# GpSimd in place of VectorE for the two 16-bit parts of the softmax shift in a fused SSM, FFN and attention kernel, with fillers in five waits of TensorE

## The chip, the cores and the metric

The kernel runs on one core of a Trainium2 chip. A core has five engines with queues of their own, each of which works through its instructions in order: TensorE (PE; its weight loads are shown as PEld), VectorE (DVE), ScalarE (ACT), GpSimd (POOL) and SyncE (SP), which here starts the DMA transfers. Engines wait for one another by semaphores. The metric is the device time of one execution in microseconds (us); lower is better.

## What is computed

The input `x` has 4096 tokens of 256 channels in float32. Four layers follow one another, each with a layer norm ahead of it and the residual added behind it: a gated recurrent block, a feed-forward block with token shift, causal attention, and the same feed-forward block again.

```python
x = x + s4_block(layernorm(x))      # gates i, f, o = sigmoid(x W + b), s = tanh(x W + b), h = f * h + i * s, y = o * h
x = x + ffn(layernorm(x))           # sigmoid(xr W_r) * (relu(xk W_k)^2 W_v), xr and xk mix a token with the one before
x = x + attention(layernorm(x))     # 16 heads of 16 channels, causal, over all 4096 tokens
x = x + ffn(layernorm(x))

# attention, for each block of queries:
scores = einsum('bhqd,bhkd->bhqk', qc, k) * scale
scores = where(causal_mask, -inf, scores)
p = softmax(scores - max(scores))
oc = einsum('bhqk,bhkd->bhqd', p, v)
```

## The kernel before

Tokens go through the feed-forward and recurrent layers in 16 units of 256. Attention is cut into 32 **steps**: `STEPS` pairs each of the 8 chunks of 512 queries with each of the 4 groups of 4 heads. Step 0 is chunk 0 with group 0, step 10 chunk 2 with group 2. Within a step, the keys are walked over in tiles of 128.

The softmax needs the largest score of a query ahead of the exponentials, and it gets it by computing the scores twice. First TensorE makes score blocks with the queries on the partitions (`max`, L1746, with the mask added by L1753 on the diagonal), and VectorE reduces each 128x512 block to one column of `span_max` (`reduce`, L1537). At the end of a step VectorE does three small things: `neg` (L1543) reduces `span_max` to `neg_max`, the negative maximum of 128 queries x 16 (four query tiles and four heads); `part0` (L1550) writes its scaled value in float16, the first part of the shift; `part1` (L1555) writes what float16 lost, the second part. `shift` on TensorE (L1761, four matmuls with an identity) turns both parts into rows, ScalarE copies them out (`shift.copy`, L1272), and four DMAs (`place`) put them below the queries in `q_stack`. The second computation of the scores (`scores`, L1778, keys on the partitions) so comes out already shifted, ScalarE exponentiates it (`exp`, L1281 and L1292), GpSimd masks the tiles on the diagonal (`mask`, L1147), and `pv` (L1799) multiplies by the values, summing in a PSUM bank of its own. `out` (L1808) and two VectorE instructions (L1561 and L1569) normalize the result.

Everything else runs between these: the projections (L1595 and L1603), transposes (L1588, L1642, L1808), tanh and copies on ScalarE (L1186 to L1265), and on GpSimd the layer norms of the middle units (L978 to L985, for the recurrent block L1037 and L1039 on top), affine steps, additions and masks.

**What sets the order.** `schedule()` is a planner that runs when the kernel is built. It plays all work through with costs (`COST`) and weights (`WORTH`), and gives out one list, `ORDER`. Each engine's program walks over that list and emits the entries that are its own, so the order on each engine is fixed. `followed()` says what an entry must come behind. `part0` and `part1` are entries of VectorE in the planner, at 180 ns each. A matmul bank in PSUM (seven of them) is claimed by TensorE when its last reader is done (`claim`). `shift` waits for `shift_ready`, and everything behind it on TensorE waits with it. `settle` on GpSimd makes an instruction wait for the end of the one before. `warm` entries put transposes of an identity (L1620, **fillers**) into long planned waits of TensorE before the first and behind the last attention work; nobody reads their result.

## Time and profile before

| | us |
|---|---|
| median of 3 runs | 1751.62 |
| lowest, highest | 1751.35, 1752.64 |
| profiled execution | 1752.51 |
| its span, first to last instruction | 1750.8 |

| engine | busy us | share of the span |
|---|---|---|
| TensorE | 1711.9 | 98% |
| VectorE | 1507.0 | 86% |
| ScalarE | 1343.5 | 77% |
| GpSimd | 687.9 | 39% |

Busy time is the union of an engine's instructions. For TensorE their ends are modelled and matmuls overlap, so a busy share near 100% does not mean that it runs at its peak. The chain is the work that ended last, followed back from the last instruction, at each step to what released it or to the instruction before it on its engine.

### The profile page before, as it was taken

Reading aid. Unit: us, or ns where it says so; the run is one execution under the profiler, and the core shown is the slowest. Engines: PE = TensorE matmul, PEld = TensorE weight load, DVE = VectorE, ACT = ScalarE, POOL = GpSimd, SP = SyncE. Lnnn points to the kernel's source line nnn. Section 1 sums busy time; section 2 is a strip of 40 time slices with the busy share of each in tenths; the row PEclk is TensorE's granted clock in tenths of the full one; section 3 lists DMA queues with packets and bytes.
Section 4 is the critical chain, followed back from the end, with each engine's and each line's share of the span. In section 5 each row is a group of like instructions: output and inputs, shape, how many; then the busy total and the mean of one; then the engine's idle time right before and its main releaser. Section 6 shows DMA issues by size and latency. Waiting matters only on the chain.

```text
span 1750.8 us, 45629 instructions
## 1 busy us (share of the span) xinstructions
PE 1711.9 (98%) x18228; PEld 641.7 (37%) x18228; DVE 1507.0 (86%) x2975; ACT 1343.5 (77%) x2796; POOL 687.9 (39%) x994
## 2 busy tenths in 40 slices
PE   8999999999999999999999999999999999999997
PEld 6654444334433333334333333333333322323224
DVE  6778978986899999998999999999999999999702
ACT  3336577767677878876888688898888899998994
POOL 3348766578572453428332625211322120102221
PEclk9999999999999999999999999999999999999999
DMA  4133121003102010020000020000002000000000
GB/s 113 53 71 60 30 43 34 19 19 61 30 18 48 13 30 13 8 48 25 6 24 2 24 32 6 18 18 2 1 19 35 18 2 6 14 1 2 14 7 13
DMA packets 57000, 43.71 MB, mean 25 GB/s; under 512 B 8788, under 2 KB 56788, under 8 KB 56788
## 3 DMA queue, kind: packets, MB, share of 16 engines
q1 hardware_dynamic: 54548, 39.75, 9.5%
q8 instruction: 144, 2.36, 0.6%
q10 hardware_dynamic: 2240, 1.05, 0.4%
q14 instruction: 68, 0.56, 0.1%
HBM read 24.00 MB, written 16.25 MB: 23 GB/s over the span
## 4 chain that ended last, share of the span: by engine, by line
PE 72%; DVE 15%; ACT 4%; POOL 3%; issue 2%; DMA 0%; ACTq 0%; POOLq 0%; DVEq 0%
PE psum L1799 22%; PE psum L1746 14%; PE psum L1778 13%; DVE span_max L1537 12%; PE psum L1595 10%; PE psum L1603 9%; ACT probs L1281 2%; PE psum L1588 2%; ACT probs L1292 1%; PE psum L1753 1%; PE psum L1808 1%; DVE rows L1476 1%; DVE small L1386 0%; POOL small L979 0%; POOL rows L985 0%
## 5 line engine op out<-in xcount | busy, mean ns | idle before, releaser
L1537 DVE TENSOR_REDUCE span_max<-psum 128x1 f32<-128x512 f32 (+3 forms) x2304 | 1313.9, 635 | 100.0 <-PE psum L1746 71.8
L1281 ACT ACTIVATE probs<-psum 128x512 f32<-128x512 f32 (+2 forms) x2178 | 1054.1, 571 | 165.9 <-PE psum L1778 162.4
L1799 PE MATMUL psum<-probs,v_aug 128*17 128x512 f32 (+3 forms) x4608 | 564.5, 562 | 1.7 <-ACT oT L1301 1.3
L1746 PE MATMUL psum<-k_stack,q_stack 48*128 48x512 f16 (+3 forms) x2304 | 528.8, 364 | 4.4 <-DVE span_max L1537 3.3
L1778 PE MATMUL psum<-q_stack,k_stack 50*128 50x512 f16 (+3 forms) x2304 | 508.3, 364 | 4.4 <-ACT probs L1292 1.2
L1778 PEld LDWEIGHTS psum<-q_stack,k_stack 50*128 50x128 f16 x2304 | 147.7, 93 | 378.6 <-ACT probs L1281 272.8
L1746 PEld LDWEIGHTS psum<-k_stack,q_stack 48*128 48x128 f16 x2304 | 154.9, 93 | 298.8 <-DVE span_max L1537 223.4
L1147 POOL TENSOR_SCALAR_AFFINE_SELECT probs<-probs 128x512 f32<-128x512 f32 x128 | 81.2, 637 | 319.0 <-ACT probs L1281 288.9
L1799 PEld LDWEIGHTS psum<-probs,v_aug 128*17 128x17 f32 x4608 | 78.2, 95 | 134.9 <-issue 114.1
L1186 ACT ACTIVATE rows<-psum,cols 128x256 f32<-128x256 f32 x128 | 53.8, 479 | 56.8 <-PE psum L1595 53.2
L1753 PE MATMUL psum<-mask_keys,mask_rows 64*128 64x64 bf16 x1024 | 93.8, 189 | 0.0
L1753 PEld LDWEIGHTS psum<-mask_keys,mask_rows 64*128 64x128 bf16 x1024 | 76.6, 95 | 28.8 <-issue 0.2
L1140 POOL TENSOR_TENSOR rows<-rows 128x512 f32<-128x512 f32 x26 | 33.1, 1273 | 108.6 <-ACT rows L1223 108.6
L1386 DVE BATCH_NORM_STATS2 small<-rows 128x6 f32<-128x256 f32 x160 | 59.3, 412 | 15.5 <-POOL rows L1124 8.3
L1595 PE MATMUL psum<-rows,w_k 128*32 128x256 f32 x1024 | 68.7, 386 | 3.3 <-DVE rows L1503 2.3
L985 POOL TENSOR_SCALAR rows<-rows,small 128x256 f32<-128x256 f32 x124 | 67.8, 554 | 6.8
L1088 POOL TENSOR_TENSOR rows<-rows 128x512 f32<-128x512 f32 x26 | 27.0, 1040 | 106.2 <-ACT rows L1200 106.2
L1603 PE MATMUL psum<-w_r,rows 128*32 128x256 f32 x1024 | 67.9, 383 | 0.7 <-POOL rows L1101 0.2
L1603 PE MATMUL psum<-w_v,rows 128*32 128x256 f32 x1024 | 67.7, 383 | 0.7 <-DVE span_max L1537 0.4
L1135 POOL TENSOR_SCALAR rows<-rows 128x512 f32<-128x512 f32 x26 | 16.4, 630 | 130.4 <-ACT rows L1207 130.3
L1561 DVE RECIPROCAL inv_sum<-psum 128x16 f32<-128x16 f32 x32 | 8.0, 250 | 67.6 <-PE psum L1808 67.2
L979 POOL TENSOR_TENSOR small<-small 128x2 f32<-128x2 f32 x80 | 57.9, 723 | 6.7
(139 smaller groups left out, 1543.7 us busy)
## 6 DMA issues: line engine op xcount, KB each, us to landing
q_stack<-q_parts SPq DMA_DIRECT2D x192, 32.0 KB, 1.9
k_stack<-k_parts SPq DMA_DIRECT2D x42, 128.0 KB, 4.8
rows<-in_x SPq DMA_DIRECT2D x16, 256.0 KB, 2.8
q_parts<-rows SPq DMA_DIRECT2D x32, 128.0 KB, 2.0
k_parts<-rows SPq DMA_DIRECT2D x32, 128.0 KB, 2.3
out<-rows SPq DMA_DIRECT2D x16, 256.0 KB, 2.2
x_rows<-rows SPq DMA_DIRECT2D x14, 256.0 KB, 2.1
rows<-x_rows SPq DMA_DIRECT2D x14, 256.0 KB, 2.7
```

Source lines behind the costliest of these rows:

```text
L979: return nc.gpsimd.tensor_tensor(rstd[:, ln], var_eps[:, ln], minus_half, ALU.pow)
L985: ins = nc.gpsimd.tensor_scalar(dst[:, j], src[:, j], neg_mean[:, ln, j:j + 1], rstd[:, ln, j:j + 1], ALU.add, ALU.mult)
L1147: nc.gpsimd.affine_select(out=tri, in_=tri, compare_op=ALU.is_ge, fill=0.0, base=0, pattern=[[0, HG], [1, P]], channel_multiplier=-1).then ...
L1281: act.activation(probs[:, tile % PROBS, i, q0:], bank(b)[:, q0:], ACT.Exp, scale=SCALE / QK_SCALE).then_inc(exp_done, 1)
L1386: ins = nc.vector.bn_stats(stats[:, ln, j], src[:, j])
L1537: nc.vector.tensor_reduce(span_max[:, s % SPAN_RING, row:row + 1, k0 // SPAN:k0 // SPAN + 1], bank(b)[:, 0:k1 - k0], AX.X, ALU.max).then_i ...
L1595: ins = nc.tensor.matmul(bank_chan(b)[c:c + COLUMNS, e], w[:, k, e * P + c:e * P + c + COLUMNS], src[:, k], start=(k == 0), stop=(k == CT ...
L1603: ins = nc.tensor.matmul(bank_tok(b)[c:c + COLUMNS, j], src[:, k, j * P + c:j * P + c + COLUMNS], w[:, k], start=(k == 0), stop=(k == CT - 1))
L1746: ins = nc.tensor.matmul(bank(b)[:, 0:k1 - k0], q_stack[row:row + SCORE_ROWS, s % Q_RING, u, qt * P:(qt + 1) * P], k_stack[row:row + SCORE ...
L1753: ins = nc.tensor.matmul(bank(b)[:, k:k + HALF], mask_rows[row:row + HALF, n], mask_keys[row:row + HALF], start=False, stop=(n == 1))
L1778: nc.tensor.matmul(bank(b)[:, q0:], k_stack[row:row + STACK, g * PAIRS + u, j * P:(j + 1) * P], q_stack[row:row + STACK, s % Q_RING, u, q0 ...
L1799: ins = nc.tensor.matmul(pv_bank[32 * h:32 * h + VW, q0:], v_aug[:, j, g * HG + h, :], probs[:, tile % PROBS, h, q0:], start=(j == 0), sto ...
```

## The change

The two parts of the shift are written by GpSimd. VectorE still computes `neg`. At the place of `part1` in the order GpSimd waits for `neg`, scales `neg_max` in place, copies it to float16 as the first part, and subtracts that from the scaled value for the second, each of the three waiting for the end of the one before. `neg` now also waits for the parts of the step before, as GpSimd reads and writes `neg_max`. The planner is not told: in it `part0` and `part1` are still two entries of VectorE, so all other work stands in the same order.

The planner also gets a second rule for fillers: a planned wait of TensorE over 300 ns, after the first `max` and before the first `pv`, gets one filler for every 110 ns beyond 190.

```diff
@@ schedule(), the planner
         if e == "PE" and gap > 1000 and (not summed or summed == len(TILES)):
             order.append(("warm", int(WARM_SHARE * (gap - 400) / (WARM if free["PE"] else WARM_COLD))))
+        elif e == "PE" and gap > 2 * SWITCH + WARM and maxed and not summed:
+            order.append(("warm", int((gap - 2 * SWITCH) / WARM)))
@@ semaphores
-        neg_ready, part_ready, shift_ready, shift_copied = (sem(n) for n in ("neg_ready", "part_ready", "shift_ready",
-                                                                              "shift_copied"))
+        neg_ready, shift_ready, shift_copied = (sem(n) for n in ("neg_ready", "shift_ready", "shift_copied"))
@@ GpSimd
+                elif op[0] == "part1":
+                    s = op[1]
+                    pool.wait_ge(neg_ready, s + 1)
+                    if s >= 2:
+                        pool.wait_ge(full["shift"], s - 1)
+                    settle(nc.gpsimd.tensor_scalar(neg_max[:], neg_max[:], 1.0 / ROW_UNIT, None, ALU.mult))
+                    settle(nc.gpsimd.tensor_copy(shift_parts[:, s % 2, :, 0], neg_max[:]))
+                    nc.gpsimd.tensor_tensor(shift_parts[:, s % 2, :, 1], neg_max[:], shift_parts[:, s % 2, :, 0],
+                                            ALU.subtract).then_inc(shift_ready, 1)
@@ VectorE
                     dve.wait_ge(span_reduced, 2 * MAXIMA_UPTO[s])
+                    if s:
+                        dve.wait_ge(shift_ready, s)
                     spans = ((STEPS[s][1] + 1) * CHUNK + SPAN - 1) // SPAN
                     nc.vector.tensor_reduce(neg_max[:], span_max[:, s % SPAN_RING, :, 0:spans], AX.X, ALU.max,
                                             negate=True).then_inc(neg_ready, 1)
-                elif op[0] == "part0":
-                    s = op[1]
-                    dve.wait_ge(neg_ready, s + 1)
-                    if s >= 2:
-                        dve.wait_ge(full["shift"], s - 1)
-                    nc.vector.tensor_scalar(shift_parts[:, s % 2, :, 0], neg_max[:], 1.0 / ROW_UNIT, None,
-                                            ALU.mult).then_inc(part_ready, 1)
-                elif op[0] == "part1":
-                    s = op[1]
-                    dve.wait_ge(part_ready, s + 1)
-                    nc.vector.scalar_tensor_tensor(out=shift_parts[:, s % 2, :, 1], in0=neg_max[:],
-                                                   scalar=1.0 / ROW_UNIT, in1=shift_parts[:, s % 2, :, 0],
-                                                   op0=ALU.mult, op1=ALU.subtract).then_inc(shift_ready, 1)
@@ TensorE, op "warm"
-                    if scores:
+                    if scores == HG * len(TILES):
                         pe.wait_ge(o_copied, len(STEPS))
                     else:
                         pe.wait_ge(pv_cleared, 1)
```

On GpSimd, in step 10 (chunk 2, third group of heads), before the change. L982 to L985 normalize a unit, L1037 and L1039 finish the recurrent block's norm, L1079 copies a column, and the next normalization follows:

```order
L982 TENSOR_SCALAR small<-small 128x2
L978 TENSOR_SCALAR small<-small 128x2
L979 TENSOR_TENSOR small<-small 128x2
L985 TENSOR_SCALAR rows<-rows,small 128x256 x2
L1037 TENSOR_TENSOR rows<-rows,gamma_b 128x512
L1039 TENSOR_TENSOR rows<-rows 128x512
L1079 COPY rows<-small 128x2
L982 TENSOR_SCALAR small<-small 128x2
```

The same place after the change (line numbers of the changed kernel, two higher):

```order
L984 TENSOR_SCALAR small<-small 128x2
L980 TENSOR_SCALAR small<-small 128x2
L981 TENSOR_TENSOR small<-small 128x2
L987 TENSOR_SCALAR rows<-rows,small 128x256 x2
L1039 TENSOR_TENSOR rows<-rows,gamma_b 128x512
L1041 TENSOR_TENSOR rows<-rows 128x512
L1127 TENSOR_SCALAR neg_max<-neg_max 128x16
L1128 CAST shift_parts<-neg_max 128x16
L1129 TENSOR_TENSOR shift_parts<-neg_max,shift_parts 128x16
L1081 COPY rows<-small 128x2
L984 TENSOR_SCALAR small<-small 128x2
```

Three instructions have come in behind the last addition of the norm and ahead of the copy; nothing else has moved.

On TensorE, between the maxima of step 0, with the difference of before and after. L1588 transposes a unit's rows, L1746 and L1753 are a `max` block and its mask, L1620 are the fillers:

```order
+L1620 MATMUL psum<-ident 128x128 x5
+L1746 MATMUL psum<-k_stack,q_stack 128x256
+L1753 MATMUL psum<-mask_keys,mask_rows 128x64 x2
+L1746 MATMUL psum<-k_stack,q_stack 128x256
+L1753 MATMUL psum<-mask_keys,mask_rows 128x64 x2
+L1588 MATMUL psum<-ident,rows 128x128 x4
+L1746 MATMUL psum<-k_stack,q_stack 128x384
+L1753 MATMUL psum<-mask_keys,mask_rows 128x64 x2
+L1746 MATMUL psum<-k_stack,q_stack 128x384
+L1753 MATMUL psum<-mask_keys,mask_rows 128x64 x2
+L1620 MATMUL psum<-ident 128x128 x3
```

The rows between the fillers also stand in the kernel before, in the same order. In all five places there are 2, 5, 3, 2 and 2 fillers, 14 together.

## Rows read from the trace of the kernel before

**Rows 1.** The page: busy time by engine; the last chain by engine.

```profile
PE 1711.9 (98%) x18228; PEld 641.7 (37%) x18228; DVE 1507.0 (86%) x2975; ACT 1343.5 (77%) x2796; POOL 687.9 (39%) x994
...
PE 72%; DVE 15%; ACT 4%; POOL 3%; issue 2%; DMA 0%; ACTq 0%; POOLq 0%; DVEq 0%
```

**Rows 2.** VectorE's groups by shape: busy us, mean ns, idle before.

```profile
L1550 DVE TENSOR_SCALAR shift_parts<-neg_max 128x16 f16<-128x16 f32 x32 | 12.3, 383 | 0.3
...
L1555 DVE SCALAR_TENSOR_TENSOR shift_parts<-neg_max,shift_parts 128x16 f16<-128x16 f32 x32 | 8.3, 259 | 0.4
```

**Rows 3.** The chain, steps 4, 5, 10 and 27: start us, us, what.

```profile
188.50 0.61 DVE shift_parts L1550
...
210.52 0.39 DVE shift_parts L1550
...
364.84 0.20 PE psum L1761 x4
...
1338.23 0.68 DVE shift_parts L1550
```

**Rows 4.** Timeline of step 13: start us, us, instruction, [idle before <-releaser].

```profile
499.29 0.22 POOL L978 TENSOR_SCALAR small<-small 128x2 f32<-128x2 f32 x1
...
499.59 0.71 POOL L979 TENSOR_TENSOR small<-small 128x2 f32<-128x2 f32 x1
...
502.94 1.26 POOL L1039 TENSOR_TENSOR rows<-rows 128x512 f32<-128x512 f32 x1
503.15 1.10 DVE L1555 SCALAR_TENSOR_TENSOR shift_parts<-neg_max,shift_parts 128x16 f16<-128x16 f32 x1
...
504.39 0.38 PE L1761 MATMUL psum<-ident_h,shift_parts 128*8 128x128 f16 x4 [1.41 <-DVE shift_parts L1555]
```

**Rows 5.** GpSimd's groups by shape.

```profile
L1101 POOL TENSOR_TENSOR rows<-rows 128x512 f32<-128x512 f32 x52 | 56.9, 1094 | 4.3
...
L982 POOL TENSOR_SCALAR small<-small 128x2 f32<-128x2 f32 x62 | 15.2, 246 | 33.3 <-DVE small L1401 19.8 <-DVE rows L1462 5.4 <-POOL rows L1110 2.9
...
L1079 POOL COPY rows<-small 128x2 f32<-128x2 f32 x32 | 6.4, 199 | 0.0
```

**Rows 6.** Timelines of TensorE and GpSimd, step 10.

```profile
364.66 0.39 PE L1761 MATMUL psum<-ident_h,shift_parts 128*8 128x128 f16 x4
...
365.87 1.09 POOL L1039 TENSOR_TENSOR rows<-rows 128x512 f32<-128x512 f32 x1
```

**Rows 7.** The same, steps 6 and 27.

```profile
234.60 1.10 POOL L985 TENSOR_SCALAR rows<-rows,small 128x256 f32<-128x256 f32 x2
...
234.91 0.39 PE L1761 MATMUL psum<-ident_h,shift_parts 128*8 128x128 f16 x4
...
1340.15 1.09 POOL L1101 TENSOR_TENSOR rows<-rows 128x512 f32<-128x512 f32 x1
...
1340.74 0.39 PE L1761 MATMUL psum<-ident_h,shift_parts 128*8 128x128 f16 x4
```

**Rows 8.** The same, step 11.

```profile
395.06 1.16 POOL L1130 TENSOR_TENSOR rows<-rows 128x512 f16<-128x512 f32 x1
...
395.39 0.39 PE L1761 MATMUL psum<-ident_h,shift_parts 128*8 128x128 f16 x4
...
397.79 1.16 POOL L1130 TENSOR_TENSOR rows<-rows 128x512 f16<-128x512 f32 x1 [1.44 <-ACT rows L1245]
```

**Rows 9.** TensorE's timeline, 88 to 113 us; a window's busy times and clock; the chain.

```profile
90.87 1.20 PE L1620 MATMUL psum<-ident 128*128 128x128 f32 x9
...
111.04 0.28 PE L1746 MATMUL psum<-k_stack,q_stack 48*128 48x256 f16 x1 [0.66 <-DVE span_max L1537]
...
core 0: us, PE busy (x) PEld busy (x) DVE busy (x) ACT busy (x) POOL busy (x), PEclk, DMA share, GB/s
...
112.30:119.10 6.80, 6.37 (x60) 3.27 (x60) 6.80 (x18) 1.09 (x2) 1.27 (x1) 0.50 0.01 2
...
114.65 4.97 PE psum L1595 x48
...
120.30 2.73 PE psum L1595 x48
```

## The prediction

> **What bounds the kernel now.** I first read the page's busy shares [rows 1]: TensorE 98%, VectorE 86%, ScalarE 77%, GpSimd 39%. A busy TensorE is not one at its peak, so I next read the chain that ended last, by engine: 72% TensorE, 15% VectorE, 3% GpSimd [rows 1]. TensorE's fixed order carries the end, with detours over VectorE where a bank waits for a maximum. A chain piece that starts when its releaser ends has no slack: delay it and the rest of the chain moves by as much. Shorten it, and only as much is won as the next-longest path allows. So each of the 32 steps is read at one place, `neg`, the two parts, and the `shift` matmuls on TensorE, and I ask whether that place is on the chain.
>
> **What VectorE gives up.** Two instructions a step go: L1550, 32 at a mean of 383 ns, 12.3 us, and L1555, 32 at 259 ns, 8.3 us; 20.6 us together [rows 2]. Off the chain this is worth nothing. Following the chain piece by piece I find 18 pieces of these two lines, the first and the last in [rows 3], about 10.5 us in sum. Their means are well over their usual length because some wait for GpSimd: in step 13 L1555 starts at 503.15 and lasts 1.10, to 504.25, while GpSimd's L1039 runs from 502.94 for 1.26, to 504.20 [rows 4]; L1550 before it took 1.15 beside L1037 in the same way. By the Trainium skill, SBUF — State Buffer, section "SBUF: two separate sides", VectorE and GpSimd share one pair of ports, which one instruction holds to its end while the other blocks. The trace agrees: the long part ends 0.05 us behind GpSimd's instruction. That rule alone would speak for the move, as it makes both parts cost nothing on VectorE.
>
> Of the ten or so steps in which the chain runs through these pieces, most need the parts for their own shift, so the path only moves over to GpSimd. In four it goes on into reductions: step 5 (0.39 for L1550 [rows 3], and 0.97 for the L1555 behind it), and steps 14, 15 and 16, read in the same way (0.64, 0.54 and 0.78). At most 1.36 + 1.96 = 3.3 us. I take 1.0 and 1.4, that is about seven tenths, because TensorE follows closely behind. **Gain 2.4 us (0 to 3.3).**
>
> **What GpSimd takes on.** Three instructions a step, with a wait between each: a tensor_scalar, a cast, a subtraction, all 128x16. The trace has none of these on GpSimd. The nearest rows are 246 ns for a 128x2 tensor_scalar, 199 ns for a 128x2 copy, 1094 ns for a 128x512 tensor_tensor [rows 5]. 128x16 lies next to the small ends: 0.26 + 0.21 + 0.28 = 0.75. The hand-over from L978 to L979 costs 499.59 - 499.29 - 0.22 = 0.08 [rows 4], twice 0.16. From the last part to TensorE it was 504.39 - 503.15 - 1.10 = 0.14 [rows 4]. So about 1.03 us pass from when GpSimd is free to when `shift` starts (0.8 at the copy's price for all three, 1.3 with one at a third of the big subtraction). Added up that is some 29 us on an engine 39% busy; mostly it hides in GpSimd's waits.
>
> What does not hide is the queue. GpSimd runs its list in order, and the parts stand where `part1` stood, behind work that in this trace is later than the plan. So `shift` starts at the end of GpSimd's preceding instruction plus 1.03, if that is later than before:
> Step 10: L1039 ends 365.87 + 1.09 = 366.96, shift 367.99 instead of 364.66: +3.3 [rows 6]. `neg` had ended 5 us before; all that time GpSimd is in two normalizations.
> Step 6: L985 ends 235.70, shift 236.73 instead of 234.91: +1.8 [rows 7].
> Step 27: L1101 ends 1341.24, shift 1342.27 instead of 1340.74: +1.5 [rows 7]. Step 21, read alike: +1.3.
> Step 13: L1039 ends 504.20, 505.23 instead of 504.39: +0.85 [rows 4].
> Step 11: L1130 ends 396.22, 397.25 instead of 395.39: +1.9. Here the chain is on GpSimd, but its next L1130 at 397.79 waits for ScalarE's L1245, which stands behind the shift's copy L1272: the delay comes through whole [rows 8].
> Five more steps, read alike: 2 (0.3), 3 (0.95, the three instructions stand directly in a chain of GpSimd's instructions), 4 (0.3), 7 (0.6), 22 (0.55).
> In the other 21 steps GpSimd is done in time, or the shift had been waiting behind other matmuls. In all 3.3 + 1.8 + 1.3 + 1.5 + 0.85 + 1.9 + 2.7 = **13.3 us lost**. `shift` is on the chain, or a bank wait from it, in each of these (step 10's piece at 364.84 is in [rows 3]), so I count them whole. Behind the waiting `shift` on TensorE stand score, maximum and value matmuls, and VectorE and ScalarE live on those. With 0.8 or 1.3 for the three instructions the sum is 10.8 or 16.3. GpSimd's masks behind the parts come up to 1.03 us later in a few steps; the value matmuls that need them come after the equally late `shift`: 0 to 1, taken as 0. The new wait of `neg` on the parts of the step before, with reductions queued behind it on VectorE, costs nothing: the parts are done in the few us named here, and two `neg` lie many reductions apart.
>
> **The fillers.** Five places get 14 transposes between them; nine in a row take 1.20 us [rows 9], so 2, 5, 3, 2 and 2 of them take 0.27, 0.67, 0.40, 0.27 and 0.27. TensorE's idle time there is 0.66 where five go [rows 9] and 0.41, 0.29, 0.26 and 0.28 in the others, counted from a matmul's modelled end, which lies 0.1 and more behind its last column, so they fit within about 0.05. So they cost nothing. What they can bring: the granted clock is 0.50, TensorE's lower level of 1.2 GHz, from 112.3 to 119.1, right behind those idle times. 48 matmuls of L1595 take 4.97 us there against 2.73 just after [rows 9]: 2.2 us, with the four transposes ahead of them 2.8 at most. But VectorE is busy for 6.80 of these 6.80 us [rows 9] and would take over as the bound: I take half, 1.4 us (0 to 2.8). By the Trainium skill, TensorE: Matmul & The Clock Gate, section "HAM oscillation — how this bites in real kernels", short idle pieces between groups of matmuls can lower the clock again, so filling them should hold it; the row of 0.50 behind the waits agrees, but no run here shows yet that these few fillers are enough.
>
> **Sum.** 1750.8 + 13.3 - 2.4 - 1.4 = 1760.3 for the span. The profiled execution took 1752.51 with a span of 1750.8, so 1.7 lies around it: 1762.0. The median of the three runs is 0.9 below that execution: **1761.0 us**, 0.54% slower.
>
> **Rivals.**
> 1. GpSimd is on time, VectorE's relief stays. The late GpSimd is that of one execution; once work starts earlier, if GpSimd's backlog at steps 6, 10, 11, 21 and 27 moves ahead of `neg`, the stalls fall and the gains stand: 1751.6 - 3.3 - 2.8 = 1745.5. For it: GpSimd is idle 61% of the span. Against it: in step 10 GpSimd has no gap worth the name in the 6 us before, and what feeds it (VectorE's statistics) does not come sooner. It decides where less than 1 us of the stalls is left. 0.10.
> 2. A draw. Only the two largest stalls, steps 10 and 11 (5.2 us), are smaller, because they hang on a backlog of one stretch, and gains are at their upper ends: 1751.6 + 8.1 - 6.1 = 1753.6. 0.18.
> 3. The clock falls in the new stall. In step 10 TensorE would stand idle for about 3 us; the 1.41 ahead of step 13's shift [rows 4] kept the clock, but at 112.3 it fell behind waits of 0.66 and less [rows 9]. A stretch like that of [rows 9] costs another 2.2 to 3.4: 1764. 0.16.
> 4. The 128x16 instructions cost 1.3 us or more: 1764 to 1766. 0.08.
> The forecast has 0.48. The range of 1753 to 1768 takes in the forecast's own ends (10.8 to 16.3 lost, 0 to 6.1 gained), rivals 3 and 4 and most of the draw. A measurement of this kernel can tell about 0.2%, 3.5 us, from no change. Faster by more than that is rival 1, 0.10; within it lies most of rival 2 and the low edge of the forecast, 0.18; slower 0.72.
>
> **What the changed profile would show.** Right: `shift` waits for GpSimd's subtraction, in steps 10, 6, 11, 13, 21 and 27 above all, for some 12 us; GpSimd's three instructions at about 0.26, 0.21 and 0.28 us; VectorE's busy time down by about 20 us with more idle time in its place; the granted clock 1.00 from 112 to 119. Wrong: small waits of `shift` for GpSimd, which would be rival 1 or 2; a second stretch of half clock behind 365 us, rival 3; or GpSimd instructions of 0.4 us and more, rival 4.

## The result and the profile after

| | before | after |
|---|---|---|
| median | 1752.13 us (4 runs) | 1771.76 us (4 runs) |
| lowest, highest | 1751.35, 1752.76 | 1770.12, 1773.39 |
| profiled execution's span | 1750.8 | 1769.3 |

The ratio is 1.0113, with a 95% interval of 1.0101 to 1.0125. The change costs 19.6 us. The forecast was a loss of 9.4 us and a range that ended at 1768: the sign was right, the size half of what came, and the time lies outside the range.

The first view is the page of the kernel after, busy time by engine; it answers to [rows 1].

```profile
PE 1716.5 (97%) x18242; PEld 642.0 (36%) x18242; DVE 1492.8 (84%) x2911; ACT 1345.0 (76%) x2796; POOL 708.5 (40%) x1090
```

VectorE lost 14.2 us of work, GpSimd gained 20.6, and TensorE has 4.6 us more on its hands although it does only 14 short transposes more. That last number is the first hint of a slower clock: the same matmuls took longer. VectorE's two instructions a step were 20.6 us; its other instructions took some 6 us longer in sum, 4.6 of them in the 128x512 reductions of `span_max` (1305.2 us before, 1309.9 after), and no run here tells why.

GpSimd's groups by shape (busy us, mean ns | idle before) show the three new instructions, which answer to [rows 5]:

```profile
L1127 POOL TENSOR_SCALAR neg_max<-neg_max 128x16 f32<-128x16 f32 x32 | 8.7, 273 | 120.8 <-DVE neg_max L1556 120.8
...
L1129 POOL TENSOR_TENSOR shift_parts<-neg_max,shift_parts 128x16 f16<-128x16 f32 x32 | 7.5, 236 | 2.7
L1128 POOL CAST shift_parts<-neg_max 128x16 f16<-128x16 f32 x32 | 6.5, 203 | 2.2
```

273, 203 and 236 ns stand where I had put 260, 210 and 280. The 120.8 us ahead of L1127 are time in which GpSimd waits for `neg`: in most steps it really is early. Who waits for the last of the three (idle us of the waiting engine, times), from the view of that one line:

```profile
L1129 POOL TENSOR_TENSOR shift_parts<-neg_max,shift_parts x32: 220/226/562, 123.9 to 1672.4; 128x16 f16<-128x16 f32 x32
...
who waited for it (us, times):
  PE psum L1761: 18.4, 13
```

So in 13 of 32 steps `shift` found GpSimd late, for 18.4 us in all. Of these 1.6 us were there before as waits for VectorE, 1.41 in step 13 [rows 4] and 0.15 in step 7; **16.8 us are new**. (A third wait of before, 0.42 us in step 4, is gone.) Nobody but `shift` waited, so the new wait of `neg` for the parts cost nothing, as forecast. The largest new one is in step 10. The timeline of that place (start us, us, instruction, [idle before <-releaser]) answers to [rows 6]:

```profile
371.02 1.26 POOL L1039 TENSOR_TENSOR rows<-rows,gamma_b 128x512 f32<-128x512 f32 x1
372.37 1.09 POOL L1041 TENSOR_TENSOR rows<-rows 128x512 f32<-128x512 f32 x1
373.43 0.28 POOL L1127 TENSOR_SCALAR neg_max<-neg_max 128x16 f32<-128x16 f32 x1
373.77 0.20 POOL L1128 CAST shift_parts<-neg_max 128x16 f16<-128x16 f32 x1
374.06 0.22 POOL L1129 TENSOR_TENSOR shift_parts<-neg_max,shift_parts 128x16 f16<-128x16 f32 x1
374.43 0.38 PE L1761 MATMUL psum<-ident_h,shift_parts 128*8 128x128 f16 x4 [3.05 <-POOL shift_parts L1129]
```

This is the forecast's picture: the two big norm instructions end at 373.46, and 0.97 us later `shift` starts, where I had said 1.03 and a loss of 3.3.

**Where the loss comes in.** Both traces have all matmuls in the same order (fillers aside), so each matmul can be set against its own twin. The table gives, for `shift`, the start after less the start before, in us:

| step | 0 | 2 | 3 | 4 | 5 | 6 | 7 | 9 | 10 | 11 | 13 | 14 | 20 | 21 | 27 | 31 |
|---|---|---|---|---|---|---|---|---|---|---|---|---|---|---|---|---|
| later by | -2.0 | -0.9 | +0.4 | +1.8 | +1.1 | +2.8 | +4.6 | +6.5 | +9.8 | +13.1 | +13.7 | +16.8 | +16.1 | +17.4 | +18.5 | +18.5 |

It is a staircase that climbs, with small steps down (0.7 us at step 5, 0.7 between steps 14 and 20). Nothing large is given back, and it ends at the 18.5 us by which the span is longer. Two kinds of step make it: the waits of `shift`, and stretches in which TensorE runs on its lower clock. The windows (us; busy us and count of each engine; granted clock; DMA share; GB/s) answer to [rows 9]:

```profile
core 0: us, PE busy (x) PEld busy (x) DVE busy (x) ACT busy (x) POOL busy (x), PEclk, DMA share, GB/s
...
112.30:119.10 6.80, 6.54 (x106) 3.54 (x107) 6.80 (x19) 1.33 (x3) 2.23 (x4) 1.00 0.01 2
188.00:191.40 3.40, 3.37 (x31) 1.63 (x28) 1.55 (x5) 1.43 (x3) 2.54 (x6) 0.50 0.29 80
239.20:242.60 3.40, 3.40 (x36) 1.35 (x32) 3.04 (x8) 2.44 (x6) 3.23 (x4) 0.50 0.01 2
375.70:379.10 3.40, 3.40 (x19) 0.58 (x15) 2.19 (x6) 2.17 (x6) 2.85 (x7) 0.50 0.06 7
519.10:522.50 3.40, 3.40 (x25) 0.86 (x21) 3.04 (x6) 3.22 (x8) 3.21 (x6) 0.50 0.01 2
```

The half clock at 112 is gone, as the fillers were meant to bring about, and four new stretches stand elsewhere. Three of them begin 1 to 2 us behind a long wait of `shift`: steps 6 (wait 1.56, shift at 237.66), 10 (3.05, at 374.43) and 13 (2.21, at 518.05). From twin to twin, TensorE falls back by 1.2, 1.3, 1.6 and 1.6 us across the four, 5.7 together, 4.5 of it behind the three waits.

The lead of 2.0 us at step 0 is not the fillers' alone. TensorE was 2.75 us early before step 0's wait of 0.67, and 1.0 of that stood at 112 us, ahead of anything that the fillers' clock could win. Most of it arises at 23 us, where the change has done nothing yet. The rows are from before and then from after:

```profile
23.37 1.97 PE L1720 MATMUL psum<-probs 128*128 128x256 f32 x8 [0.80 <-DVE probs L1332]
...
22.66 1.97 PE L1720 MATMUL psum<-probs 128*128 128x256 f32 x8
```

`e4_clock_fill`, which up to there is the same program as the kernel after, waits 1.15 us at this place, so it is scatter between executions. From 112 to 120 us the lead grows from 1.0 to 2.75, and 1.7 us is what the held clock wins. In sum: scatter -1.0, fillers -1.7, waits +16.8, clock +5.7, and -1.3 for VectorE's relief and all that I can't assign make the 18.5.

### The profile page after: what moved, and what is told of

It is laid out like the page before. It is cut to its first block and busy times, and to the rows that moved or that the text cites. A ratio compares the mean times of both kernels' runs of the same rounds, so it can differ in the third digit from the quotient of the medians.

```text
span 1769.3 us, 45720 instructions
## 1 busy us (share of the span) xinstructions
PE 1716.5 (97%) x18242; PEld 642.0 (36%) x18242; DVE 1492.8 (84%) x2911; ACT 1345.0 (76%) x2796; POOL 708.5 (40%) x1090
## 3 DMA queue, kind: packets, MB, share of 16 engines
q10 hardware_dynamic: 2240, 1.05, 0.4%
## 5 line engine op out<-in xcount | busy, mean ns | idle before, releaser
L1746 PE MATMUL psum<-k_stack,q_stack 48*128 48x512 f16 (+3 forms) x2304 | 528.6, 364 | 2.7 <-DVE span_max L1548 1.6
L1746 PEld LDWEIGHTS psum<-k_stack,q_stack 48*128 48x128 f16 x2304 | 154.4, 94 | 296.0 <-DVE span_max L1548 219.3
L1753 PE MATMUL psum<-mask_keys,mask_rows 64*128 64x64 bf16 x1024 | 94.0, 189 | 0.0
L1753 PEld LDWEIGHTS psum<-mask_keys,mask_rows 64*128 64x128 bf16 x1024 | 76.8, 96 | 29.6 <-issue 0.3
L1151 POOL TENSOR_TENSOR rows<-rows 128x512 f32<-128x512 f32 x26 | 33.1, 1274 | 103.3 <-ACT rows L1234 103.3
L1146 POOL TENSOR_SCALAR rows<-rows 128x512 f32<-128x512 f32 x26 | 16.1, 618 | 115.6 <-ACT rows L1218 115.5
L1100 POOL TENSOR_SCALAR rows<-rows,small,cols 128x256 f32<-128x256 f32 x104 | 58.4, 570 | 1.1
```

The source lines that it names most:

```text
L1100: ins = nc.gpsimd.tensor_scalar(dst[:, k], f_xr[:, k], zero, cols[:, COL[om], k:k + 1], ALU.add, ALU.mult)
L1746: ins = nc.tensor.matmul(bank(b)[:, 0:k1 - k0], q_stack[row:row + SCORE_ROWS, s % Q_RING, u, qt * P:(qt + 1) * P], k_stack[row:row + SCORE ...
L1753: ins = nc.tensor.matmul(bank(b)[:, k:k + HALF], mask_rows[row:row + HALF, n], mask_keys[row:row + HALF], start=False, stop=(n == 1))
```

## The experiments

Theory: `shift` stands in TensorE's fixed order behind GpSimd's in-order queue, each wait comes through whole, and the clock that falls behind the longer waits is a second loss of its own. Rivals: the fillers cost rather than help; VectorE's new order is what costs; or the parts are late for GpSimd's price, not for its place in the queue. Times are medians; ratios are against runs of the kernel before on the same chip in the same job. Where a step is given as late or early, that is the difference in the start of its `shift` to the profiled kernel before, as in the table above.

### The two halves of the change apart

`e1_fillers_only` is the kernel before with the new rule for fillers alone:

```diff
+        elif e == "PE" and gap > 2 * SWITCH + WARM and maxed and not summed:
+            order.append(("warm", int((gap - 2 * SWITCH) / WARM)))
...
-                    if scores:
+                    if scores == HG * len(TILES):
```

> The kernel before with the 14 fillers alone; VectorE writes both parts. Theory (four terms: late GpSimd, clock lost behind the stalls, fillers' gain, little relief): the granted clock stays 1.00 from 112 to 119 us, and the kernel comes out about 1.9 us faster than before, 1750.2 us, by the difference of the two traces at step 0's shift (-2.0 us). Rival (the gain at 112 us is given back later, as VectorE or GpSimd bounds the stretch behind it): within 0.5 us of before.

Measured: 1751.44 us (10 runs) against 1752.51 (19 runs), ratio 0.9997 (0.9987 to 1.0007), so nothing that can be measured. Its windows:

```profile
112.30:119.10 6.80, 6.55 (x106) 3.57 (x108) 6.80 (x20) 1.26 (x3) 2.16 (x4) 1.00 0.01 2
...
184.70:188.10 3.40, 3.37 (x25) 1.56 (x26) 2.20 (x6) 1.48 (x4) 2.20 (x3) 0.50 0.38 106
```

The clock holds at 112, and TensorE then is 2.75 us early through steps 0 to 3, 1.0 of it from before the clock's share, as in the kernel after. A half-clock stretch that the kernel before did not have follows at 185, and at step 4 the lead is 1.75, from step 10 on 1.2 to 1.5. The fillers work where they stand; part of what they win is lost again, and the rest is small against how the kernel before scatters by itself (1749.9 to 1753.9 in these 19 runs). By the time the rival was right, though what gave the gain back was the clock and not another engine.

`e2_parts_only` is the kernel after without that rule. 

> The changed kernel without the five groups of fillers; GpSimd writes both parts. Theory: the loss of the changed kernel (+19.6) plus the fillers' gain of 1.9, so about +21.5 against before, 1773.6 us, with a half-clock stretch at about 112 us again. Rival (the fillers only move the phase of the clock, and it is their doing that it falls at 188, 239, 376 and 519 us): those four stretches are gone, and the kernel is about 5 us faster than the changed one, 1766.

Measured: 1770.04 us (4 runs), ratio 1.0104 (1.0088 to 1.0119), within the interval of the full change. Half clock stands at 111.7 to 118.5, as before, and at 190.2, 241.4, 374.5 and 517.9. Both expectations missed: the kernel is neither 2 us slower than the changed one nor 5 faster. The stretches behind steps 6, 10 and 13 belong to the parts on GpSimd, not to the fillers, and the whole loss is the parts'. The waits of 1.31 and 1.16 us in steps 9 and 14 are not there, nor is step 0's; the section on the prediction comes back to them.

### What the parts cost at all

`e5_no_parts` is `e1_fillers_only` in which nobody writes the parts: VectorE fills both once with zeros, and `shift` waits for `neg` alone. It leaves the two part instructions of all 32 steps out, so its scores are not shifted.

```diff
+            nc.vector.memset(shift_parts[:], 0.0).then_inc(filled, 1)
...
-                elif op[0] == "part0":
...
-                elif op[0] == "part1":
...
-                                            negate=True).then_inc(neg_ready, 1)
+                                            negate=True).then_inc(shift_ready, 1)
```

> The kernel of e1 (fillers alone) with both parts left out: nobody writes them, shift reads zeros, and neg alone releases it, so the scores are exponentiated unshifted. VectorE is relieved of the same two instructions a step and GpSimd gets nothing. Theory (the relief is worth little, because TensorE follows closely behind VectorE): 0.5 to 3 us faster than e1, 1748.5 to 1751. Rival (my 10.5 us of chain pieces are worth their length once no queue of GpSimd takes their place): 8 us or more faster, below 1744.

Measured: 1745.52 us (5 runs) against 1751.94 (15), ratio 0.9963 (0.9949 to 0.9977). No half clock anywhere; the last `shift` is 6.96 early. So to write the parts costs some 6 us against `e1_fillers_only`, and in this order no placing of them on another engine should bring more. That lies between what the two sides had expected, and above the 3.3 us that my prediction gave as the upper bound of VectorE's relief. Of the 5.7 us between the two traces, 1.0 is the stretch at 185 of `e1_fillers_only`, which is not there, and 1.4 the wait of step 13, gone with the parts. The bound counted only the steps in which the chain goes on into reductions, but where the chain goes through the parts into `shift`, leaving them out wins as well. That part is not to be had by moving them: GpSimd's three instructions take 1.0 us of their own there.

### Price or place

`e8_one_more` casts twice, which adds 0.28 us (0.20 and a hand-over) to each step on GpSimd and changes no order:

```diff
-                    settle(nc.gpsimd.tensor_copy(shift_parts[:, s % 2, :, 0], neg_max[:]))
+                    for _ in range(2):
+                        settle(nc.gpsimd.tensor_copy(shift_parts[:, s % 2, :, 0], neg_max[:]))
```

> The changed kernel with the cast on GpSimd done twice, so one more instruction of 0.20 us and one more hand-over of 0.09 us in each step. Theory (the queue position decides, the arithmetic only adds its own length in the 13 steps where shift waits): 13 x 0.29 = 3.8 us slower than the changed kernel, 1775.5, give or take a half-clock stretch of 1 to 2 us. Rival (GpSimd's backlog builds up from instruction to instruction, so small work is multiplied): over 8 us slower than the changed kernel.

Measured: 1775.54 us (4 runs), ratio 1.0139 (1.0124 to 1.0154), 3.8 us over the kernel after, as expected. The trace shows that the agreement is in part luck. In ten of the thirteen late steps the wait is 0.25 to 0.28 us longer, so there the price counts in full. In steps 2, 9 and 14 it is shorter (by 0.56, 1.04 and 0.09), and all waits of `shift` for GpSimd together rose by 1.2 us only, to 19.6. The clock's share is another one too: there are five stretches, at 137.2, 239.6, 372.7, 410.3 and 1362.6, the third 6.9 us long, and none behind step 13, where the wait was longer than in the kernel after:

```profile
520.79 0.38 PE L1762 MATMUL psum<-ident_h,shift_parts 128*8 128x128 f16 x4 [2.46 <-POOL shift_parts L1130]
...
519.00:524.00 5.00, 3.21 (x37) 1.19 (x37) 2.25 (x5) 2.76 (x7) 4.35 (x12) 1.00 0.00 1
```

`e3_parts_at_neg` keeps the price and changes the place. GpSimd's three instructions move to where `neg` stands in the common list, some entries earlier:

```diff
-                elif op[0] == "part1":
+                elif op[0] == "neg":
```

> The changed kernel with GpSimd's three instructions moved up in GpSimd's order to the place of neg, ahead of the one or two entries (a mask, a 5 us z.norm in step 10, an addition) that the order has between neg and part1 in 19 of the 32 steps. Theory (the loss is GpSimd's queue, not its arithmetic): the idle time ahead of shift goes in steps 3, 4, 6, 9, 10, 14 and 27 and shrinks in 2, 7, 11 and 22; it stays in 13 and 21, where the z.norm stands ahead of neg. Stalls fall from 17 to about 5 us, the clock falls at most once or twice, and the kernel takes about 1755. Rival (GpSimd now waits for neg with its own late work behind it, and that hurts as much): 1765 or more.

Measured: 1755.79 us (10 runs), ratio 1.0016 (1.0007 to 1.0026). Some 16 of the 19.6 us are back (17 by the ratios), by a change of one word. Step 10 on GpSimd's timeline, ahead of the two norm instructions now and not behind them:

```profile
363.07 0.28 POOL L1127 TENSOR_SCALAR neg_max<-neg_max 128x16 f32<-128x16 f32 x1
...
366.62 1.28 POOL L1039 TENSOR_TENSOR rows<-rows,gamma_b 128x512 f32<-128x512 f32 x1
367.97 1.09 POOL L1041 TENSOR_TENSOR rows<-rows 128x512 f32<-128x512 f32 x1
```

The waits in steps 2, 3, 6, 9, 10, 14, 22 and 27 are gone. Left are 0.68 in step 0, 0.19 in 7, 0.48 in 11, 1.06 in 21 and, the largest, step 13:

```profile
507.47 0.38 PE L1761 MATMUL psum<-ident_h,shift_parts 128*8 128x128 f16 x4 [2.19 <-POOL shift_parts L1129]
```

That one is followed by one of this kernel's two half-clock stretches, at 508.5. The other, from 136.5 to 143.3, begins with an idle time of 1.22 us, which is the rival's effect in one place: GpSimd writes step 1's parts ahead of a mask now, and `pv` waits for the mask.

```profile
137.82 1.91 PE L1799 MATMUL psum<-probs,v_aug 128*17 128x512 f32 x8 [1.22 <-POOL probs L1158]
```

TensorE goes from 1.8 us early at step 0 to 1.4 late at step 1, which is most of what is left of the loss. So the place in the queue makes most of the loss; the price of the three instructions counts where the place makes them late, with the same three instructions standing earlier the kernel is 3.3 us slower than before, not 19.6.

### Does the clock cost by itself

`e7_step10_only` takes `e1_fillers_only` and gives GpSimd the parts of step 10 alone, at `part1`'s place. One stall, and nothing else changed but that `neg` waits for the parts of the step before:

```diff
@@ GpSimd
+                elif op[0] == "part1" and op[1] == 10:
...
@@ VectorE
+                elif op[0] in ("part0", "part1") and op[1] == 10:
+                    pass
```

> The kernel of e1 with GpSimd writing the parts in step 10 alone, behind its z.norm as in the changed kernel; VectorE writes them in the other 31. Theory (a stall on the chain comes through whole, and the clock falls behind it): one idle time of about 3 us ahead of step 10's shift, +3.2 us at that shift and +1.2 for one half-clock stretch at about 370 us, and nothing given back until the end: 4.4 us slower than e1, 1755.8. Rival (VectorE and ScalarE catch up during the stall, and TensorE gets the time back later): under 1.5 us slower than e1.

Measured: 1757.81 us (5 runs), ratio 1.0035 (1.0021 to 1.0048), 6.4 us over `e1_fillers_only`, 2 more than expected. The stall and the window behind it:

```profile
366.47 0.28 POOL L1127 TENSOR_SCALAR neg_max<-neg_max 128x16 f32<-128x16 f32 x1
...
367.48 0.58 PE L1776 MATMUL psum<-ident_h,shift_parts 128*8 128x128 f16 x4 [3.08 <-POOL shift_parts L1129]
...
366.50:373.30 6.80, 5.82 (x32) 1.50 (x36) 2.80 (x7) 3.30 (x7) 5.35 (x15) 0.50 0.14 39
```

The step before, `shift` was 0.44 early; in step 10 it is 2.82 late, in step 11 5.45, and at the last step 5.35. The stall costs 3.3 us, the clock behind it 2.6 more (the clock had fallen at 366.5, still within the stall, and stayed down for 6.8 us), and in the 21 steps that follow nothing of it comes back. Another 0.8 us against `e1_fillers_only` stands already at step 9, ahead of the stall, and is not the parts'. This is the prediction's third rival in a pure form.

`e4_clock_fill` and `e11_clock_fill_all` are the kernel after with transposes that nobody reads in front of the waiting `shift`, so that TensorE works while it waits, in three steps and in eleven (of the thirteen late ones, all but 0 and 14):

```diff
                     claim(b, shift_copied, s + 1)
+                    for n in range({6: 12, 10: 26, 13: 18}.get(s, 0)):
+                        nc.tensor.transpose(bank(b)[:, 0:P], ident[:], ident[:])
```

(In `e11_clock_fill_all` the numbers are 2: 8, 3: 8, 6: 12, 7: 5, 9: 8, 10: 26, 11: 13, 13: 18, 21: 8, 22: 8, 27: 15.) They do nothing for the parts, which `shift` waits for as before.

> The changed kernel with 12, 26 and 18 transposes ahead of TensorE's wait for the parts in steps 6, 10 and 13, written into the bank that shift then overwrites. They fill the stalls and take no work away. Theory (three of the four half-clock stretches are caused by these idle times and cost 1.4, 1.2 and 2.0 us): the clock stays 1.00 at 239, 376 and 519 us and the kernel is about 4.6 us faster than the changed one, 1767.2. Rival (the stalls alone cost the time and the clock costs nothing, since VectorE or ScalarE bound those stretches): 1771.8, unchanged.

Measured: 1765.55 us (4 runs), ratio 1.0074 (1.0059 to 1.0089), 6.2 us better than the kernel after. Its windows over the three places:

```profile
239.00:243.00 4.00, 4.00 (x64) 2.08 (x63) 3.64 (x9) 3.34 (x8) 3.83 (x6) 1.00 0.03 6
371.00:380.00 9.00, 9.00 (x99) 4.40 (x97) 4.21 (x11) 5.53 (x12) 8.05 (x17) 1.00 0.11 31
512.00:520.00 8.00, 8.00 (x88) 4.40 (x83) 3.89 (x9) 4.94 (x11) 7.19 (x17) 1.00 0.13 31
...
1353.90:1357.30 3.40, 3.38 (x30) 1.30 (x34) 1.67 (x4) 1.82 (x4) 0.43 (x1) 0.51 0.03 7
```

Three stretches are gone, one at 190.0 stayed, and one at 1353.9, in step 27, is new. The gain is above the 4.6 us expected for the clock; in this trace step 14's wait of 1.16 us is not there and step 9's is 0.86 instead of 1.31, with nothing filled in either.

> The changed kernel with fillers ahead of TensorE's wait for the parts in all eleven steps with a stall on the chain (2, 3, 6, 7, 9, 10, 11, 13, 21, 22, 27), in place of the three of e4. Theory (with the clock held the loss is the sum of the stalls alone, and e4's two stretches at 190 and 1354 us were stalls not filled): no half-clock stretch behind 150 us apart from perhaps the one at 190, 1.5 to 2.5 us faster than e4, 1.0062 of before. Rival (the fillers themselves delay shift by the last of them in each step): as e4 or slower.

Measured: 1763.72 us (4 runs), ratio 1.0072 (1.0057 to 1.0087), with one stretch of half clock left, at 187.5. Step 10 on TensorE, and the one window that stayed:

```profile
368.96 3.06 PE L1760 MATMUL psum<-ident 128*128 128x128 f32 x26
...
372.03 0.39 PE L1763 MATMUL psum<-ident_h,shift_parts 128*8 128x128 f16 x4
...
187.50:190.90 3.40, 3.31 (x33) 1.39 (x33) 2.31 (x7) 1.71 (x4) 3.25 (x7) 0.50 0.20 57
```

The 129 transposes that nobody needs, 26 of them in step 10, make the kernel faster. Against the kernel after, 0.41% are won, 7.2 us (the two intervals together leave some 3 us to either side); in the traces the span is 7.5 shorter. Not all of that is the clock: from twin to twin 4.6 us lie in the three stretches, 1.2 are the wait of step 14, which is not there in this trace either, and the rest are small waits. By the times it can't be told from `e4_clock_fill`. What is left is the loss of the other stalls: 0.72%, 12.6 us (10.0 to 15.2), or 11.0 at the last `shift` of the trace.

### A version that uses what was learnt

`e6_split_at_neg` has the fillers, GpSimd's parts at `neg`'s place, and VectorE as before in steps 0, 1, 13 and 21, where `e3_parts_at_neg` still waited or GpSimd was behind:

```diff
@@ GpSimd
+                elif op[0] == "neg" and op[1] not in (0, 1, 13, 21):
...
@@ VectorE
+                elif op[0] in ("part0", "part1") and op[1] not in (0, 1, 13, 21):
+                    pass
```

> The kernel of e3 (GpSimd's three instructions at neg's place), but in steps 0, 1, 13 and 21, where e3 still showed TensorE idle ahead of or around shift, VectorE writes the parts as before. Theory (what is left of the loss in e3 are those queues and the clock lost behind them): the +2.9 us of e3 against before go, and the kernel comes to e1 or up to 1.5 us below it, 1750 to 1751.5. Rival (GpSimd's waits for neg cost something spread over all steps): it stays at 1753 or more.

Measured: 1749.52 us (10 runs), ratio 0.9988 (0.9979 to 0.9997), no half clock anywhere. The page, and the one wait for GpSimd that counts, in step 11:

```profile
PE 1710.0 (98%) x18242; PEld 642.1 (37%) x18242; DVE 1496.1 (86%) x2919; ACT 1343.8 (77%) x2796; POOL 706.6 (40%) x1078
...
394.22 0.38 PE L1776 MATMUL psum<-ident_h,shift_parts 128*8 128x128 f16 x4 [0.50 <-POOL shift_parts L1129]
```

It is the fastest of all versions that compute everything, by 2.1 us against the kernel before. That is less than the 3.5 us (0.2%) that I set as the line for "no change", though the interval lies just under 1. It overlaps that of `e1_fillers_only` (0.9987 to 1.0007), so no run shows that the parts on GpSimd win anything over the fillers alone.

`e9_split2` gives VectorE step 11 too:

> The kernel of e6, with VectorE writing the parts in step 11 as well, where e6 still showed 0.50 us of idle TensorE ahead of shift and lost 1.3 us against the step before. Theory (the chain there runs through ScalarE's shift copy, so the loss comes through whole): about 1.0 us faster than e6, 0.998 of before. Rival (something else costs it there): no difference from e6.

Measured: 1749.57 us (10 runs), ratio 0.9988 (0.9978 to 0.9997). From step 10 to 11 it loses 0.66 us instead of 1.3, but a stretch of half clock at 185.8 comes with it, and the time is the same.

`e10_split_no_fillers` is `e6_split_at_neg` without the rule for fillers:

> The kernel of e6 without the five groups of fillers. Theory, after e1 and e2 had shown less than 0.1% for the fillers: they decide where the clock dips, not by how much in sum; within 0.1% of e6. Rival (their gain of 2 us at 112 us is real here, since e6's trace has no half-clock stretch at all): 2 to 3 us slower than e6, and a half-clock stretch at about 112 us.

Measured: 1750.69 us (10 runs), ratio 0.9998 (0.9988 to 1.0007). The half clock of the kernel before is back:

```profile
111.50:118.30 6.80, 6.34 (x60) 3.20 (x60) 6.80 (x18) 1.03 (x2) 1.28 (x1) 0.50 0.01 2
```

The step from `e10_split_no_fillers` to `e6_split_at_neg` is 1.2 us, about the 1.4 that my prediction gave to the fillers, but the two intervals overlap, so it is an indication and no more. In the traces TensorE wins 2.2 us up to step 0 by the fillers' clock, after 1.0 us of scatter at 23.7 us the other way.

## Why the prediction was half right

The forecast's terms beside what the traces show, in us of the span:

| | forecast | measured |
|---|---|---|
| waits of `shift` | +13.3 | +16.8 |
| clock, four new stretches | 0 | +5.7 |
| VectorE's relief and all that is not assigned | -2.4 | -1.3 |
| fillers, at 112 us | -1.4 | -1.7 |
| scatter ahead of 112 us | 0 | -1.0 |
| sum | +9.5 | +18.5 |

**What bounds the kernel: right.** TensorE's fixed order carries the end, and `shift` is on it. `e7_step10_only` shows it: from step 9 to step 31 `shift` goes from 0.44 us early to 5.35 late, 5.8 us for one stall of 3.3 and the clock's 2.6, none given back.

**The cost of the instructions: right.** 1.0 us from the start of the first to `shift`, forecast 1.03.

**The late steps: right in kind, three missed, two much too small.** The named ones, forecast and measured wait:

| step | 10 | 6 | 11 | 27 | 21 | 13 | 3 | 7 | 22 | 2 | 9 | 14 |
|---|---|---|---|---|---|---|---|---|---|---|---|---|
| forecast | 3.3 | 1.8 | 1.9 | 1.5 | 1.3 | 0.85 | 0.95 | 0.6 | 0.55 | 0.3 | 0 | 0 |
| measured, new | 3.05 | 1.56 | 1.61 | 1.79 | 1.05 | 0.80 | 1.10 | 0.57 | 1.09 | 1.08 | 1.31 | 1.16 |

For the large ones the method holds within 0.3 us. Step 4, forecast at 0.3, had no wait; step 0 had one of 0.67. What failed here is that in the other 21 steps GpSimd should be done in time, for which I had read GpSimd's timeline as it stood. Step 2 is late by more than its 0.3 because step 1's three instructions had already pushed GpSimd's queue back: the instruction ahead of them starts 2.0 us earlier than before (138.65 against 140.63), GpSimd has no gap from there on, and the mask ahead of step 2's parts ends only 1.2 earlier (147.21 against 148.38). `shift` starts at 148.18 behind a wait of 1.08. Steps 9 and 14 are late for another reason. In both GpSimd's addition L1121, which stands ahead of the parts, waits for a reload of rows (start us, us, instruction, [idle before <-releaser]):

```profile
326.37 0.38 SPq L924 DMA_DIRECT2D rows<-x_rows  x1
...
329.58 1.27 POOL L1121 TENSOR_TENSOR rows<-rows,bo_b 128x512 f32<-128x512 f32 x1 [1.99 <-DMA rows<-x_rows]
...
338.38 0.33 PE L1761 MATMUL psum<-ident_h,shift_parts 128*8 128x128 f16 x3 [1.31 <-POOL shift_parts L1129]
...
567.18 1.27 POOL L1121 TENSOR_TENSOR rows<-rows,bo_b 128x512 f32<-128x512 f32 x1 [1.95 <-DMA rows<-x_rows]
...
570.55 0.38 PE L1761 MATMUL psum<-ident_h,shift_parts 128*8 128x128 f16 x4 [1.16 <-POOL shift_parts L1129]
```

In the kernel before, that addition did not wait in step 9, and step 14's reload took 2.55 us against 4.35 now. The late reload is not the parts' doing: in `e1_fillers_only` step 14's took 4.31 us, and GpSimd waited for it as long, but there the parts were on VectorE and `shift` was not late.

```profile
550.20 1.27 POOL L1121 TENSOR_TENSOR rows<-rows,bo_b 128x512 f32<-128x512 f32 x1 [1.91 <-DMA rows<-x_rows]
```

In `e2_parts_only` it took 2.73 us and neither step had a wait of `shift`. So these two stalls, 2.5 us, come and go between executions. The parts had been put into a queue that also waits for DMAs, and I had looked at what GpSimd does there but not at what it waits for. In sum the waits are 16.8 us against 13.3.

**VectorE's relief: too small to see.** Forecast 2.4 us. The staircase steps down by 0.7 at step 5, as named, and TensorE makes good 0.7 us within 1 us of step 21's stall and 0.6 behind step 22's. New waits for VectorE's reductions go the other way, 0.7 at 186.7 us and 0.4 at 267.8. The balance is 1.3, and how much of it is the relief stays open.

**The fillers: right at their place, not in the time.** The clock was 1.00 from 112 to 119, and that won 1.7 us up to step 0 where I had taken 1.4. But `e1_fillers_only`, with a new stretch at 185, differs from the kernel before by nothing that can be measured.

**The clock behind the stalls: this is the step that failed.** I had set it apart as a rival, with one stretch behind step 10, a chance of 0.16 and 2.2 to 3.4 us, and left it out of the sum. It came three times behind waits of `shift`, 4.5 us, and a fourth stretch whose cause is open added 1.2. `e7_step10_only` shows 2.6 us for one stretch behind a single stall. In `e11_clock_fill_all`, with three of the four gone and one stall fewer, the loss is 12.6 us (10.0 to 15.2) against the forecast's 9.4, and its 1763.7 lies inside the range that I had given; without those transposes it is 19.6 and outside. The waits, 3.5 us above the forecast, are the second part of the miss. The evidence was there: [rows 9] show the clock at 0.50 behind waits of 0.66 us and less, and the sum itself added four waits of 1.5 us and more. That step 13's 1.41 us of wait kept the clock [rows 4] was one row against it, and I let it decide. The Trainium skill, TensorE: Matmul & The Clock Gate, section "HAM oscillation — how this bites in real kernels", tells of a kernel whose waits for DMAs recur between its groups of matmuls and make TensorE pay the slower clock each time anew. The waits there are 3 to 5 us long; the trace agrees in kind, with its stretches behind the 1.56, 3.05 and 2.21 us of steps 6, 10 and 13, but not each time, as steps 11 (1.61) and 27 (1.79) show none. What I had taken from that section in the prediction, that short idle pieces can lower the clock, stands in the same page's next one, "A second HAM failure mode: psum-queue depth-cycling". I had used it only for what the fillers would win, not for what the new waits would lose.

The stretch at 188 is not explained. It is there with the parts on VectorE (`e1_fillers_only`, 184.7) and on GpSimd, with and without fillers, and not in `e3_parts_at_neg`, `e5_no_parts`, `e6_split_at_neg`, `e8_one_more`, `e10_split_no_fillers` or the kernel before. In the kernel after a wait of 0.99 us for VectorE's reduction stands ahead of it, at 186.72; `e8_one_more` has the same wait of 0.99 us and keeps the clock. No run tells what decides it.

## What to carry to other kernels

Work that moves to another engine starts when what stands ahead of it in that engine's queue has ended, and that includes what those instructions wait for, DMAs too; the idle share of the engine (61% here) tells nothing of it. So put it ahead of the long entries, and leave it where it was in the steps where that can't be done: a change of place alone (`e3_parts_at_neg`) gave back some 16 of 19.6 us, and the split version came out 0.12% ahead of the kernel before, no more than the fillers alone could explain. And where a change puts new waits on TensorE, count the slower clock behind each of the longer ones as a term of the sum, here 2.6 us on top of a stall of 3.3; if the wait can't be avoided, transposes that nobody reads save most of that part (4.6 of the 5.7 us).

## What the hardware showed that I had not expected

The clock fell behind single waits of 1.56 to 3.08 us within otherwise dense work, and stayed down for 3.4 us in some places and 6.8 in others (3.4 behind step 10 in the kernel after, 6.8 behind the same stall in `e7_step10_only`). The same length of wait does not always do it: 1.79 us in step 27 left the clock alone in the kernel after, while in `e4_clock_fill` a stretch begins there, at 1353.9; and 2.21 us in step 13 were followed by a stretch in the kernel after, 2.46 us in `e8_one_more` were not.

An early lead can be lost to such a stretch: the kernel with fillers alone was 2.75 us ahead at step 0 and 1.23 at the end.

One and the same reload of 256 KB (step 14's, `rows<-x_rows`) took 2.55 us from its issue to its landing before, 4.35 after, 4.31 in `e1_fillers_only` and 2.73 in `e2_parts_only`. What stands behind it in an in-order queue inherits that.
